# Product and silu at the head of a pair's slot, scaled results and turned products at its end

## What is computed

```
def _L1_ffn_ref(hidden_states, W_A, W_B, W_up, W_down):
    E, K, H, F, R = (8, 2, 128, 256, 64)
    gate_hidden = jnp.einsum('nh,erh->ner', x, W_A)
    scores = jnp.sqrt(jnp.sum(gate_hidden * gate_hidden, axis=-1))
    topk_scores, topk_idx = jax.lax.top_k(scores, K)
    topk_w = jax.nn.softmax(topk_scores, axis=-1)
    g = jnp.einsum('ner,efr->nef', gate_hidden, W_B)
    up = jnp.einsum('nh,efh->nef', x, W_up)
    y = jnp.einsum('nef,ehf->neh', jax.nn.silu(g) * up, W_down)
    out = jnp.einsum('neh,ne->nh', y, w_full)
xn = _layernorm(x)
x = x + _L1_attn_ref(xn, ...) + _L1_ffn_ref(xn, ...)
```

## Time and profile before

| what | value |
|---|---|
| median of three runs | 655.79 us (652.28 to 659.21) |
| profiled execution | 649.94 us, span of its trace 648.1 us |
| PE busy | 567.0 us, 87% |
| DVE busy | 447.0 us, 69% |
| ACT busy | 300.8 us, 46% |
| POOL busy | 298.2 us, 46% |
| slots of pairs 0 to 35 (first to last `gate_up`) | 447.07 to 624.9 us |
| end: last results stored, read back and added | 624.9 to 648.1 us |

### The profile page before, as it was taken

The page is one execution under the profiler, slowest core; times in us unless marked ns, Lnnn a source line. Parts: engine busy times, 40 slices in busy tenths (PEclk is TensorE's granted clock), DMA queues, the critical chain, the costliest instruction groups (busy, mean ns, idle before and its releaser), DMA issues.

```text
span 648.1 us, 10568 instructions
## 1 busy us (share of the span) xinstructions
PE 567.0 (87%) x3218; PEld 467.6 (72%) x3218; DVE 447.0 (69%) x1199; ACT 300.8 (46%) x558; POOL 298.2 (46%) x268
## 2 busy tenths in 40 slices
PE   5899999989899998999999999986877877888870
PEld 2879985667687677888888878765665666777660
DVE  6858998729721992344659989987787685656673
ACT  4460247655424441344577657855835433334230
POOL 5610030006561563265334458768344755666661
PEclk9999999999999998999999999997999799999995
DMA  7350031400023502133222232122211232322626
GB/s 215 128 243 17 2 129 33 97 9 2 21 110 110 172 0 65 59 93 94 75 67 79 70 100 79 39 99 68 56 55 59 59 89 71 82 73 67 208 74 223
DMA packets 48381, 54.94 MB, mean 85 GB/s; under 512 B 7029, under 2 KB 40374, under 8 KB 47271
## 3 DMA queue, kind: packets, MB, share of 16 engines
q1 hardware_dynamic: 43542, 42.99, 21.2%
q0 software_dynamic: 4320, 8.99, 4.1%
q10 hardware_dynamic: 466, 2.31, 1.6%
HBM read 36.22 MB, written 15.94 MB: 80 GB/s over the span
## 4 chain that ended last, share of the span: by engine, by line
PE 30%; DVE 12%; issue 9%; ACT 6%; POOL 4%; another core or an unknown queue 4%; DMA 2%; SPq 1%; POOLq 0%; ACTq 0%; DVEq 0%
PE banks L1762 4%; PE banks L1764 4%; PE banks L1763 4%; PE banks L1968 3%; PE banks L1882 2%; PE banks L2119 2%; PE banks L1874 2%; POOL arena L888 1%; PE banks L2104 1%; PE banks L1895 1%; PE banks L1896 1%; DVE arena L1606 1%; DMA arena<-result_rows 1%; PE banks L2075 1%
## 5 line engine op out<-in xcount | busy, mean ns | idle before, releaser
L873 POOL DMA_INDIRECT result_rows<-arena x71 | 69.3, 975 | 38.8 <-PE banks L1764 16.6
L858 POOL DMA_INDIRECT expert_rows<-arena x64 | 63.6, 994 | 40.6 <-issue 14.6
L822 POOL TENSOR_TENSOR arena<-arena 128x512 f32<-128x512 f32 x32 | 40.8, 1275 | 86.2 <-DVE arena L1431 86.2
L888 POOL TENSOR_TENSOR arena<-arena 128x512 f32<-128x512 f32 x32 | 42.4, 1325 | 68.2 <-DVE arena L1585 68.1
L1585 DVE TENSOR_TENSOR arena<-banks,arena 128x512 f32<-128x512 f32 x48 | 33.0, 688 | 42.5 <-PE banks L1764 33.5
L1968 PEld LDWEIGHTS banks<-arena 128*128 128x128 f32 x384 | 48.8, 191 | 6.9 <-POOL arena L888 3.0
L1968 PE MATMUL banks<-arena 128*128 128x128 f32 x384 | 51.6, 277 | 1.9 <-DVE arena L1585 1.1
L1874 PE MATMUL banks<-arena 128*128 128x512 f32 x96 | 50.5, 608 | 2.4 <-DVE arena L1431 1.1
L1882 PEld LDWEIGHTS banks<-arena 128*128 128x128 f32 x256 | 33.0, 191 | 19.0 <-POOL arena L822 14.4
L2119 PE MATMUL banks<-arena 128*128 x284 | 39.6, 284 | 7.4 <-DVE arena L1628 4.0
L1087 ACT ACTIVATE rows_hi<-banks 128x256 fp32r<-128x256 f32 (+1 forms) x36 | 13.6, 379 | 67.7 <-remote 33.6
(11 more groups left out here) (281 smaller groups left out, 1628.7 us busy)
## 6 DMA issues: line engine op xcount, KB each, us to landing
arena<-expert_weights SPq DMA_DIRECT2D x64, 128.0 KB, 3.4
arena<-expert_rows SPq DMA_DIRECT2D x71, 66.0 KB
arena<-in_x SPq DMA_DIRECT2D x8, 512.0 KB, 6.8
arena<-result_rows SPq DMA_DIRECT2D x8, 512.0 KB
arena<-in_dft_f SPq DMA_DIRECT2D x1, 2048.0 KB, 9.6
normed_hi<-xnt_hi SPq DMA_DIRECT2D x1, 2048.0 KB, 6.4
normed_lo<-xnt_lo SPq DMA_DIRECT2D x1, 2048.0 KB, 10.9
arena<-in_dft_i SPq DMA_DIRECT2D x1, 2048.0 KB, 7.7
```

What stands on the lines that cost most here:

```text
L822: nc.gpsimd.tensor_tensor(out=T1[:, q % 3, :], in0=T1[:, q % 3, :], in1=T2[:, q % 2, :], op=ALU.add).then_inc(y_in, 1)
L858: pool.indirect_dma_start(out=xrows, out_offset=bass.IndirectOffsetOnAxis(ap=SLOT[:, k, t:t + 1], axis=0), in_=XNF[:, t, :], in_offset=Non ...
L873: pool.indirect_dma_start(out=yrows, out_offset=bass.IndirectOffsetOnAxis(ap=DEST[:, i, n:n + 1], axis=0), in_=YB[:, i % YBUFS, n, :], in_ ...
L888: nc.gpsimd.tensor_tensor(out=AM0[slot % 2], in0=AM0[slot % 2], in1=WB0[:, m, :], op=ALU.mult).then_inc(weighted, 1)
```

## The change

On ACT `silu_pair(i)` moves from behind the early slots' chores and the attention copy to right behind `rows_hi(i + 1)`, and `turned(i - 1)` moves from right behind silu to the end of the slot, behind the exponentials. On DVE `product(i)` moves to right behind `rows_lo(i + 1)`, and `result_rows(i - 2)` moves to the end of the slot's work, with only `combine` behind it. Nothing is added or removed on any engine, and PE, POOL and SP keep their order.

```
@@ scalar @@
                 if 0 <= i + 1 < NP:
                     rows_hi(i + 1)
+                if 0 <= i < NP:
+                    silu_pair(i)
                 if m == 1 and st < NCH:
...
                     if step == 2:
                         attention_copy(n)
-                if 0 <= i < NP:
-                    silu_pair(i)
-                if 1 <= i <= NP:
-                    turned(i - 1)
...
                         nc.scalar.activation(e, e, ACT.Exp).then_inc(rt_exp, 1)
+                if 1 <= i <= NP:
+                    turned(i - 1)
@@ vector @@
                 if 0 <= i + 1 < NP:
                     rows_lo(i + 1)
+                if 0 <= i < NP:
+                    product(i)
                 c = due(slot, 1)
...
                 if 0 <= i < NP:
-                    product(i)
                     places_of(i)
-                if 2 <= i < NP + 2:
-                    result_rows(i - 2)
...
                             tables(bt, part)
+                if 2 <= i < NP + 2:
+                    result_rows(i - 2)
                 if i >= BACK_AT:
```

More of the change, by code:

```diff
@@ L1159, in _ @@
                         attention_copy(n)
[L1160 to L1163, removed]
                 c = due(slot, 13)
```

## The result

The changed kernel takes 658.2 us in the median of 20 runs (654.06 to 664.26), the kernel before 652.11 in 20 runs beside it (647.22 to 659.21). The ratio is 1.0097, with a 95% interval of 1.0070 to 1.0125: slower by some 6 us. The forecast was 657.5 us against 655.79, a loss of 1.7 us. The sign and the range hold; the size is under-forecast more than threefold. That 657.5 lies so near 658.2 is luck: it was counted from a median of three runs, 655.79 us, and the twenty have 652.11, 3.7 us less.

The account below looks back on a forecast made before the run. No engine was full, so order and waits were taken to bound the kernel. 9.2 - 1.0 - 4.2 + 0.3 - 2.6 = +1.7 us, on the median of 655.79 gave 657.5 us, range 649 to 666 us.

Parts of the forecast that it names:

- (a): Slots 13 to 34, DVE: product ahead of attention's division delays sixteen answers PE waits for; +9.2 us, bounds 0 and 11.8.
- (b): Slots 24 and 30, DVE: product passes L1659, so the next `gate_up` waits some 0.5 us less each time; -1.0 us.
- (c): Attention's slots: new gaps on PE should bring its next completions to ACT in time; -4.2 us, bounds 0 and -14.
- (d): Slot 2: product and silu delays, +2.6 us, mostly won back by slot 8; net +0.3 us, bounds -1 and +2.6.
- (e): Slot 9, ACT: `query_parts` and the exponentials' block use idle time ahead of `turned(8)`; -2.6 us, bounds 0 and -3.7.
- `result_rows` at no cost: End of DVE's slot: `down_rows` reads them one slot later, behind a `gate_up` of 1.6 us, so the move costs nothing.
- `turned` behind the exponentials: Slot 9, ACT: `turned(8)` and PE's `turn_products(9)` come 1.4 us later, but both end before silu(10).
- rival "slower": Attention's slots: completions stay late whatever gaps there are, and late copies delay DVE; +8.7 us, 664.5 us; chance 0.25.
- The faster one: ACT's late copies: the gaps on PE clear all ten; -8.1 us, 647.7 us; chance 0.20.
- the hidden one: PE is really behind its records, so later attention answers cost nothing and gaps win nothing; -3.3 us, 652.5 us; chance 0.15.
- The rule weighed: Slot 28: computed product ends would mean PE really works in the 1.9 us before ACT's copy; prediction held the row against it.

Follow-up runs that it names:

- e5: The kernel before, unchanged, run again on chip B for its trace: 630.96 us in one run.
- e6: The changed kernel, unchanged, run again on chip B: 648.88 us, ratio 1.0287 to the kernel before.
- e7: The changed kernel with the product at its old place in slot 2 alone, chip B: 644.49 us, ratio 1.0280 to the kernel before.
- e8: The changed kernel with the product at its old place in slot 2 and from slot 13 on, chip B: 634.71 us, ratio 1.0050 to the kernel before.
- e11: The kernel before with only `turned` moved to the end of ACT's slot, chip C: 647.67 us, ratio 1.0007.
- e12: The kernel before with only `result_rows` moved to the end of DVE's slot, chip C: 647.27 us, ratio 0.9963.
- e2: The kernel before with only the two DVE moves, product and result rows, chip A: 647.22 us, ratio 1.0255.
- e3: The kernel before with only the product moved, directly behind `rows_lo`, chip A: 643.33 us, ratio 1.0211.
- e1: The kernel before with only the two ACT moves, `silu_pair` and `turned`, chip A: 631.8 us, ratio 1.0015.

## Why the prediction was right, and where not

(a), (b) and (c), slots 13 to 35. Together +4.0 was forecast and +3.8 came. That is right as a sum and half right as a reason. Right: L1650 behind the product makes PE wait in attention, and "remote" falls to less than half. The waits forecast as 12 to 16 us came to 13.8, but that was a weak sign, since the same count gives 10.8 us before: in the first pair they grew by 3.0 us, on B from 3.6 to 13.8. Wrong in (a) is the size of the step: the 0.65 to 0.74 us were read in slots where a late completion had already held DVE back. Where completions are prompt the answer moves by 1.87 us (slot 22 of e5 and e6), and the stretch 13 to 35 grows from 96.45 to 111.01 us, 14.6, of which 5.1 lie in slots 31 and 32. Whether the upper bound of (a), 11.8, holds there stays open: the 14.6 are above it, the 9.8 us between e7 and e8 below. Wrong in most of (c) is that the gaps would bring the next completions in time. It came true in slot 20 only: behind a gap of 1.23 us in slot 19 the copy was in time, and slot 20 went from 5.50 to 5.12 us, its own later answer included. Slot 26 went from 6.27 to 6.46, slot 32 from 6.77 to 6.91, and slots 22 and 28 from 5.32 to 5.33 and from 5.24 to 5.37. Slot 26 of the changed kernel, timeline of PE and ACT:

```profile
582.47 0.76 PE L2140 MATMUL banks<-arena 128*128 128x144 f32 x4 [0.68 <-issue]
583.06 0.38 PE L2076 MATMUL banks<-arena 128*128 128x128 f32 x2
...
585.94 0.38 ACT L1087 ACTIVATE rows_hi<-banks 128x256 fp32r<-128x256 f32 x1 [1.08 <-remote]
```

The new gap is there (0.68 us), and the turned rows, done at 583.44 by PE's record, still reach ACT 2.5 us later. Gaps do not bring completions in time by rule; that the pattern I took from the first trace is a cause was not borne out. So +4.0 against +3.8 is luck in part: late completions covered much of (a), and (c) won less than forecast, and on B, where nothing is late, neither holds. (b) was right in sign, at half its size: slots 24 and 30 fell by 0.2 us each (4.23 to 4.00, 4.24 to 4.04), not 0.5.

(d), slot 2, is the largest miss. The delay itself was right (+2.6 foretold; `down_rows(0)` came 2.5 later). "By slot 8 most is won back" failed: +2.6 stayed, and e6 against e7 has 2.9. Even the +2.6 is flattered by slot 5, which took 7.57 us in the first trace of before and 5.62 after; in e5 it takes 5.82. Not foreseen was that PE then runs at a granted clock of 0.5; between 460 and 470 us that gave 43 products in 9.53 busy us instead of 51 in 8.59.

(e), slots 9 to 12, failed. The 2.96 us won up to slot 12 are near the 2.6 foretold by luck: only 0.5 came by `gate_up(11)`, and the other 2.5 in slot 11, from the clock. The step that failed is that the block would use the idle time: the late completion now stood ahead of `turned(7)`, and so ahead of the block. And 2.46 were lost in slot 12. In the earlier trace rows the 0.79 us of `gate_up(11)`'s first product, 0.48 in the earlier trace rows, already showed the lower clock, and the prediction has no term for it. On B ACT had no late completion to win from, and slots 8 to 13 took 23.58 us against 23.02. On C, e11 has 26.80 and e12 30.05 for that stretch: single late completions move it by 3 us whichever order stands.

`result_rows` at no cost: e12 (0.9963) bears it out on C; the 3.9 us between e2 and e3 on A are the open point.

Silu and `turned`: `turned` behind the exponentials was priced at 1.4 us without effect; PE waits 8.7 us for L1101 in the changed kernel and 2.70 at once in e1. In the time of the whole kernel e1 and e11 show no loss.

The rival "slower" (+8.7) had the better size for the wrong reason: its condition, that "remote" stays, did not come. The faster one (647.7) is out, since four waits on "remote" remain, and the hidden one (652.5), since PE did wait longer in attention. The rule weighed (the Trainium skill, "Perfetto Trace Analysis", section "Tensor Engine Instruction (MATMUL, LD_WEIGHTS)", by which the profiler computes the end of a product) can be set against B. In e5 PE's completions follow the computed ends within 0.2 us but for two of 203 (between 440 and 625 us, from the semaphore events), and slot 23 has nearly the same length in e5 (4.37 us) as in the first trace of before (4.32). So here the computed ends agree with the completions, and the delay seen on the other chips most likely comes after them.

Open: what makes PE's completions late, by over 0.3 us in 70 to 90 of 195 cases in the first trace of before (by how events and records are paired), on some chips and not on others. Nothing in the kernel decides it, since the same kernel had both. Open too are the 0.9 us behind slot 35, and whether e8's last 0.5% is ACT's moves.

No kernel beat the one before by more than the measurement tells; e12 at 0.9963, with an interval that ends at 1.0000, comes nearest.

## What to carry to other kernels

On an engine that works in order, what another engine waits for goes ahead of work that must itself wait: the product's 0.6 us made attention's answer 1.9 us later, since the answer behind it paid its wait for silu too. Read the price of a move in a slot where nothing else is late, because a stall that lies beside it hides it, and on a chip without the stall the price shows in full (1.0097 with it, 1.0287 on B without). And price a gap on TensorE with the work after it: the time at the lower granted clock can cost as well. A stretch at that clock that one trace has and the other hasn't can also look like the gain that was foretold, as in slot 11.

## What the runs showed of the hardware

The same kernel took 629 to 631 us on two chips and 649 to 652 on others, at about the same granted clock (0.975 in e5, 0.973 in the first profile of the kernel before). The difference lies in the pairs' part: slots 8 to 13 took 23.02 us in e5 and 29.73 in the first trace of before, slots 13 to 35 took 96.45 and 107.13. There PE's completions reached ACT late and in bunches; on A and B only one to three of some 200 were late.

PE's granted clock was 0.5 behind gaps of 1.40 us (e7), 2.81 us (e6) and 3.54 us (e6 and the changed kernel). It stayed at 1.00 behind gaps of 1.10 us (e5), of 1.62 and 2.19 us (e6, slot 22 and at 501.92 us) and of 2.23 us (before). So the length of a gap alone doesn't tell whether the clock falls.
